# Routing half 0 inside half 1's MLP, a shorter ranking, and fillers paced by scatters: one change to an adaLN block with a mixture of experts

## The reference, cut to what matters

```python
h = _layernorm(x) * (1 + ca) + sa
xn = rmsnorm(h, norm1_w)
left = gelu(xn @ left_W + left_b)
right = rg_lru(causal_depthwise_conv(xn @ right_W + right_b), ...)
x1 = left * right @ out_W + out_b + h
x1n = rmsnorm(x1, norm2_w)
mlp = gelu(x1n @ up1_W + up1_b) * (x1n @ up2_W + up2_b) @ down_W + down_b   # 256 -> 768 -> 256
x = x + ga * (mlp + x1)                                 # called x2 here
h = _layernorm(x) * (1 + cb) + sb                       # called h2 here
logits = h @ gate_w                                     # 8 experts, the best 2 of each token
combined = sum over e of cw[:, e] * (gelu(h @ w1[e] + b1[e]) @ w2[e] + b2[e])   # 256 -> 1024 -> 256
x = x + gb * (combined + h)
```

## Time and profile before

| | us |
|---|---|
| runs shown: lowest, median, highest | 304.69, 307.43, 307.59 |
| the profiled execution, its own time | 304.61 |
| its span (first to last instruction) | 302.9 |
| PE busy | 274.6 (91%) |
| DVE busy | 194.0 (64%) |
| ACT busy | 186.3 (61%) |
| POOL busy | 113.0 (37%) |

### The profile page before, as it was taken

One profiled execution on the slowest core, in us unless ns is written; L12 is line 12 of the kernel. 1 busy time (PEld: TensorE's weight loads), 2 busy tenths in 40 slices (PEclk: granted clock), 3 DMA queues, 4 the chain that ended last, 5 costly groups with the idle time before them and its releaser, 6 DMA issues.

```text
span 302.9 us, 4493 instructions
## 1 busy us (share of the span) xinstructions
PE 274.6 (91%) x1607; PEld 231.5 (76%) x1607; DVE 194.0 (64%) x450; ACT 186.3 (61%) x303; POOL 113.0 (37%) x97
## 2 busy tenths in 40 slices
PE   0799999899999999997798979999999999999980
PEld 0695546378588888785476979999999999999980
DVE  4866737929927365978392676768686867686520
ACT  5166679784296335755851869494949494959200
POOL 6000000000124123507475400838475656657562
PEclk9999999999999999999759999999999999999997
DMA  7970000000004766432135943675758392918133
GB/s 240 381 221 0 2 1 0 0 2 0 0 2 153 233 170 123 86 126 92 54 98 170 285 169 112 210 198 179 232 156 255 126 286 87 280 10 209 26 40 38
DMA packets 32727, 38.26 MB, mean 126 GB/s; under 512 B 7989, under 2 KB 28333, under 8 KB 32685
## 3 DMA queue, kind: packets, MB, share of 16 engines
q1 hardware_dynamic: 26816, 29.90, 31.7%
q0 software_dynamic: 4928, 7.44, 11.0%
q10 hardware_dynamic: 956, 0.59, 0.7%
HBM read 31.96 MB, written 8.90 MB: 135 GB/s over the span
## 4 chain that ended last, share of the span: by engine, by line
PE 41%; ACT 4%; issue 2%; DVE 1%; DMA 1%; POOL 1%; POOLq 1%; another core or an unknown queue 0%; ACTq 0%; DVEq 0%
PE bank L892 17%; PE bank L913 14%; PE bank L657 3%; PE bank L878 2%; PE bank L908 2%; PE bank L907 2%; PE bank L802 1%; DMA out_x<-y_tok,meta 1%; ACT own L1208 1%; POOL out_x L1828 1%; POOLq L188 1%; ACT hT L1086 1%; ACT own_raw L1202 1%; DVE xe_lo L1669 0%; ACT L1105 0%
## 5 line engine op out<-in xcount | busy, mean ns | idle before, releaser
L1828 POOL DMA_INDIRECT out_x<-y_tok,meta x24 | 51.0, 2127 | 50.5 <-DVE y_tok L1691 43.9
L913 PE MATMUL bank<-w_hi,own 128*128 128x256 f32 x256 | 47.9, 285 | 0.0
L892 PE MATMUL bank<-xe_hi,w_hi 128*128 128x320 f32 x128 | 39.7, 310 | 3.3 <-DVE xe_lo L1669 3.3
L1673 DVE TENSOR_TENSOR own<-own_raw,own 128x256 fp32r<-128x256 f32 x64 | 27.2, 425 | 23.3 <-ACT own L1208 17.9
L913 PEld LDWEIGHTS bank<-w_hi,own 128*128 128x128 f32 x256 | 40.4, 191 | 0.4
L1202 ACT ACTIVATE own_raw<-bank,b1c 128x320 f32<-128x320 f32 x64 | 33.9, 529 | 9.7 <-PE bank L892 9.7
L892 PE MATMUL bank<-xe_lo,w_hi 128*128 128x320 f32 x128 | 39.6, 309 | 0.0
L892 PE MATMUL bank<-xe_hi,w_lo 128*128 128x320 f32 x128 | 39.6, 309 | 0.0
L913 PE MATMUL bank<-w_lo,own 128*128 128x256 f32 x128 | 36.2, 283 | 0.0
L1208 ACT ACTIVATE own<-own_raw 128x320 fp32r<-128x320 f32 x64 | 28.7, 460 | 0.0
L1818 POOL DMA_INDIRECT gb_rows<-gb_table,meta x24 | 23.4, 974 | 11.6 <-issue 6.7
(11 more groups left out here) (226 smaller groups left out, 626.9 us busy)
## 6 DMA issues: line engine op xcount, KB each, us to landing
e_raw<-in_L_ffn_w SPq DMA_DIRECT2D x16, 1024.0 KB
x_rows<-in_L_attn_x SPq DMA_DIRECT2D x1, 2560.0 KB
xe_tok<-x_rows SPq DMA_DIRECT2D x8, 256.0 KB
raw_m<-in_L_attn_up_W SPq DMA_DIRECT2D x2, 768.0 KB, 9.9
x_tok<-in_L_attn_x SPq DMA_DIRECT2D x2, 512.0 KB, 5.0
out_x<-x_tok SPq DMA_DIRECT2D x1, 1024.0 KB
wmod<-in_L_wmod SPq DMA_DIRECT2D x1, 768.0 KB, 12.2
raw_m<-in_L_attn_down_W SPq DMA_DIRECT2D x1, 768.0 KB, 13.1
```

Source lines behind the costliest of these rows:

```text
L892: ins = nc.tensor.matmul(bank[b][:, 0:CAP], l, r, start=(c == 0 and t == 0), stop=(c == KD - 1 and t == 2))
L913: ins = nc.tensor.matmul(bank[b][0:n, 0:D], l, r, start=(c == 0 and t == 0), stop=(c == KE - 1 and t == 2))
L1673: nc.vector.tensor_tensor(own_lo[e % 2][:, f, :], own_raw[:, f % 4, 0:whole], own_hi[e % 2][:, f, 0:whole].bitcast(F32), ALU.subtract)
L1828: nc.gpsimd.indirect_dma_start(out_rows, bass.IndirectOffsetOnAxis(ap=ids[0:n, e, k, E:E + 1], axis=0), y_tok[e % 2][0:n, k, :], None, com ...
```

## The change

Six things are changed together.

1. Half 0's routing is written between half 1's `up` products: on TensorE its x2 rows and logits go from behind up(1, 2) to behind up(1, 1), its xh2 turns from behind up(1, 5) to behind up(1, 3), its h2 rows and places from between the two down products to ahead of up(1, 5). On ScalarE the root, the x2 copies, the modulation, exp and the h2 copies go between the gelus 7 to 11; on VectorE stats, norm, logits, choice, weights and slots between `v_of(7)` and `v_of(11)`. The last low part of v moves from GpSimd to VectorE, and w1's low part for expert 0 from behind `v_of(7)` to behind the weights of half 1.
2. The base of x2 (bias and x1, scaled by ga, plus x) is made ahead by `rest_of_x2`, so that behind a down product only one operation a batch is left; the transposes wait for the batch they need.
3. The ranking takes three operations instead of five: a difference, a comparison with `margin` (just below 2^-120 or -2^-120, which settles ties) and the sum.
4. Block 0's x2 rows, its logits and the weights' turn (`turn_weights(0)`) are issued ahead of the last chunk of the last down product.
5. Half 1's xh2 banks hold a batch each instead of a channel block: batch 2 is modulated by VectorE, batch 3 by ScalarE behind exp. Places stand between the two. The scatters' semaphores are one for each 128 tokens, and GpSimd waits for the half of the copied rows that it sends.
6. The 4 and the 30 fillers become 18 in six groups of three, one behind each of half 1's four a scatters and two of its b scatters; the 11 become 10.

```diff
+            def rest_of_x2(hf):
+                for dt in range(KD):
+                    until_drained(("xr", hf, dt))
+                    for q in range(BH):
+                        bb = hf * BH + q
+                        cs = slice(bb * S, (bb + 1) * S)
+                        st.mark(nc.vector.tensor_scalar(tmp[:, 2 + dt, q * S:(q + 1) * S], hT[:, dt, cs], C("down_b", dt), M(GA, dt, bb), ALU.add, ALU.mult))
+                    st.need(st.n)
+                    st.mark(nc.vector.tensor_tensor(xT[:, dt, hs[hf]], xT[:, dt, hs[hf]], tmp[:, 2 + dt, :], ALU.add))
+                return st.n
...
-                    nc.vector.scalar_tensor_tensor(out=tmp[:, 2 + dt, :], in0=ps[:], scalar=C("down_b", dt), in1=hT[:, dt, hs[hf]],
-                                                   op0=ALU.add, op1=ALU.add).then_inc(drained[b], 1)
-                    until_drained(("down", hf, dt))
...
-                        ins = nc.vector.scalar_tensor_tensor(out=xs, in0=tmp[:, 2 + dt, q * S:(q + 1) * S], scalar=M(GA, dt, bb), in1=xs,
-                                                             op0=ALU.mult, op1=ALU.add)
+                        nc.vector.scalar_tensor_tensor(out=xs, in0=ps[:, q * S:(q + 1) * S], scalar=M(GA, dt, bb), in1=xs,
+                                                       op0=ALU.mult, op1=ALU.add).then_inc(drained[b], 1)
...
-                st.mark(nc.vector.tensor_tensor(beats, other, mine, ALU.is_gt))
-                st.link(nc.vector.tensor_tensor(ties, other, mine, ALU.is_equal))
+                st.link(nc.vector.tensor_tensor(beats, other, mine, ALU.subtract))
                 dve.wait_ge(ident_done, 3)
-                st.link(nc.vector.tensor_tensor(ties, ties, before[:].rearrange("p (t e) o -> p t e o", t=1).to_broadcast([P, TH, E, E]), ALU.mult))
-                st.link(nc.vector.tensor_tensor(beats, beats, ties, ALU.add))
+                st.link(nc.vector.tensor_tensor(beats, beats, margin[:].rearrange("p (t e) o -> p t e o", t=1).to_broadcast([P, TH, E, E]), ALU.is_gt))
...
+            down(1, [0])
+
+            def first_rows():
+                x2_and_logits(1, 0)
+                turn_weights(0)
+            down(1, [1], first_rows)
             x2_and_logits(1, 1)
...
+            for n in range(TH):
+                pe.wait_ge(a_scattered[TH + n], 16)
+                stay_busy(("paced", n), any_w1, 3)
+            for n in range(BH):
+                pe.wait_ge(b_scattered[TH + n], 16)
+                stay_busy(("paced", TH + n), any_w1, 3)
...
+            def modulate_last():
+
+                b, ps = full(("xh2", 1, 1))
+                for dt in range(KD):
+                    nc.scalar.activation(hT[:, dt, T - S:T], ps[:, dt * S:(dt + 1) * S], ACT.Identity,
+                                         scale=M(CB, dt, B - 1), bias=M(SB, dt, B - 1)).then_inc(drained[b], 1)
...
             ln_root(4)
             norm2(1)
-            modulate2(1)
             numerators(1)
+            modulate_last()
             keep_h2(1)
+            keep_weights(1)
             keep_x2(1)
```

More of the change, by code:

```diff
@@ L15 @@
 CAP = 320
+TIE = 2.0 ** -120
+BELOW_TIE = TIE * (1 - 2.0 ** -24)
 class Order:
@@ L122, in take_down @@
         for dt in range(KD):
-            order.take(("down", hf, dt))
+            order.take(("down", hf, dt), drains=2)
     def take_x2t(hf):
@@ L155, in adaln_block, with take_at @@
     take_up(1, 1)
-    take_up(1, 2)
     take_x2t(0)
     order.take(("logits", 0))
+    take_up(1, 2)
     take_up(1, 3)
+    take_xh2(0)
     take_up(1, 4)
-    take_up(1, 5)
-    take_xh2(0)
-    order.take(("down", 1, 0))
     take_h2t(0)
     order.take(("places", 0))
-    order.take(("down", 1, 1))
-    take_x2t(1)
+    take_up(1, 5)
+    take_down(1)
+    for p in range(2):
+        order.take(("x2t", 1, p))
     order.take(("logits", 1))
     order.take(("cwT", 0))
-    order.take(("busy", 1), drains=0, bank=6)
-    order.take(("xh2", 1, 0), drains=2, bank=6)
-    order.take(("xh2", 1, 1), drains=2)
-    order.take(("places", 1))
-    order.take(("busy", 3), drains=0, bank=4)
-    order.next = 1
-    order.take(("h2t", 1, 0))
-    order.take(("h2t", 1, 1), bank=4)
-    take_biases(0)
-    order.take(("cwT", 1))
-    take_biases(1)
-    order.take(("busy", 2), drains=0)
+    first_bank = order.next
+    def take_at(key, n, drains=1):
+        order.take(key, drains=drains, bank=(first_bank + n) % 8)
+    take_at(("busy", 1), 0, 0)
+    take_at(("xh2", 1, 0), 0, KD)
+    take_at(("places", 1), 1, 2)
+    take_at(("xh2", 1, 1), 2, KD)
+    take_at(("h2t", 1, 0), 7)
+    take_at(("h2t", 1, 1), 6)
+    take_at(("cwT", 1), 0)
+    take_at(("b2", 0, 0), 1)
+    take_at(("b2", 0, 1), 2)
+    take_at(("b2", 1, 0), 6)
+    take_at(("b2", 1, 1), 7)
+    for n in range(TH + BH):
+        take_at(("paced", n), 3, 0)
     for j in range(4):
@@ L719, in up, with down @@
                 product(("up2", hf, m), wm(1, KD)(m), split_of(n_hi, n_lo, hf), KD)
-            def down(hf, dts=range(KD)):
+            def down(hf, dts=range(KD), between=None):
                 wm_ready(3)
@@ L743, in x2_and_logits, with bank_of @@
             def x2_and_logits(hf, dt):
-                pe.wait_ge(x2_done, KD * hf + dt + 1)
-                for p in range(2):
-                    b, ps = begin(("x2t", hf, p)) if dt == 0 else (order.at[("x2t", hf, p)][0], bank[order.at[("x2t", hf, p)][0]])
+                def bank_of(key):
+                    return begin(key) if dt == 0 else (order.at[key][0], bank[order.at[key][0]])
+                lb, logits = bank_of(("logits", hf))
+                for p in range(BH):
+                    until_drained(("down", hf, dt), p + 1)
+                    b, ps = bank_of(("x2t", hf, p))
                     for q in range(2):
@@ L1161, in all_experts @@
             def all_experts():
-                b, n, _ = order.at[("busy", 2)]
+                b, n, _ = order.at[("paced", TH + BH - 1)]
                 act.wait_ge(filled[b], n)
@@ L1592, in slots @@
                 nc.vector.tensor_scalar(slot_b[:, ts], high[:, ts], -1.0, None, ALU.add).then_inc(slots_done, 1)
+                if hf == NH - 1:
+                    until_drained(("places", hf), 2)
+                    nc.vector.tensor_scalar(overflow[:], most, float(CAP), None, ALU.is_gt).then_inc(overflow_done, 1)
             def w1_lo_of(e):
@@ L1642, in _ @@
             centre(1)
+            b, ps = full(("xh2", 1, 0))
+            for dt in range(KD):
+                nc.vector.tensor_scalar(hT[:, dt, BH * S:(BH + 1) * S], ps[:, dt * S:(dt + 1) * S], M(CB, dt, BH), M(SB, dt, BH), ALU.mult, ALU.add).then_inc(drained[b], 1)
             slots(1)
             weights(1)
+            w1_lo_of(0)
             for hf in range(NH):
```

153 lines of the change are left out of this document (81 added, 72 removed).

## The result

| | before | after |
|---|---|---|
| median of the executions | 307.24 us (304.69 to 307.59, four) | 303.07 us (301.15 to 304.09, four) |
| ratio, 95% interval | | 0.9896, 0.9856 to 0.9936 |
| the profiled execution | 304.61 us, span 302.9 | 303.28 us, span 301.5 |
| mean granted clock in it | 0.976 | 0.958 |

The kernel is faster by 1.0% (0.6 to 1.4). The forecast was 300.8 us, by a shift of 3.9 us. The medians differ by 4.2, the ratio makes 3.2 of 307.2, and the two profiled executions differ by only 1.3. In this document medians are of all executions, and ratios leave out slow ones, more than 1.5% above the kernel's fastest (five of e3's ten, one each of e4, e5 and f2; the profiles of e3 and e5 show such executions).

What follows compares the result with a forecast made beforehand. TensorE-bound expert loop taken as unchanged, so only its start counted: shifts a to e moved the turn of expert 0's rows from 163.88 to 160.0, -3.9; 304.61 - 3.9 = 300.7, said 300.8 us; own range 299 to 302.2, overall 298.3 to 305.3.

Steps and rivals of the forecast that it cites:

- term d: First scatter of half 1 on GpSimd: w1's low part beside it on VectorE costs +1.2 us, bounds 0 and +1.5.
- step e: Load and fillers: load at 155.2, rows in at 160.0, fillers ended before; turn at 160.0 instead of 163.88, -3.9 together.
- a: Until half 1's x2 rows stand in PSUM: pauses and tail change by -0.3 us, bounds -1.0 and +1.5.
- b: Ranking on VectorE: three linked operations instead of five take 1.38 us instead of 2.13, so -0.75.
- c: From the last of `centre` to the weights: exp right behind the normalising, 2.9 us instead of 5.19, so -2.3.
- rival 2: Ahead of slots: the old 3.17 us wait at L1581 comes back, c gives back 2 to 3, 303.2 us; 16%.
- Rival 1, the clock: Granted clock still down when the dense loop starts: 1.7 to 5.1 us lost, taken as 2.6, 303.4 us; 25%.
- Rivals 3 and 4: 3: w1 load or base late, 302.8 us, 6%; 4: down product starved by half 0's slow ranking, 308.7, 5%.
- Rival 5: Slow table switches ahead of gelu 11 on ScalarE: gelu and down product 2.6 us later, 303.3 us; 2%.
- The signs of being wrong: Prediction wrong if the clock is 0.50 behind 160 us, or L1541's last pair ends after 138.

Runs made afterwards that it cites:

- e3: Changed kernel with six times five fillers in one bunch of 30 instead of eighteen waiting for scatters: median 304.86 us, ratio to before 0.9876.
- e4: Changed kernel without the paced fillers (one is left): median 304.63 us, ratio to before 0.9968.
- e5: e1 with 5 fillers behind the turn of expert 0's rows and 8 behind that of expert 1's: median 300.42 us, ratio to before 0.9791.
- f2: Changed kernel with two fillers for each scatter instead of three, 12 in all: median 303.29 us, ratio to before 0.9911.
- f1: The changed kernel itself, unaltered, run and profiled a second time: median 302.01 us, ratio to before 0.9885.
- e7: Changed kernel with both blocks of half 1 modulated on ScalarE and exp behind them again: median 305.23 us, ratio to before 0.9978.
- e2: e1 with expert 1's w1 load held until ScalarE has copied out half 1's weights: median 302.06 us, ratio to before 0.9883.
- e1: Changed kernel with expert 0's w1 low part moved back between the two updates of half 1's xT: median 302.40 us, ratio to before 0.9882.
- e8: Kernel before with only the fillers changed, eighteen in threes waiting for scatters instead of thirty: median 306.46 us, ratio to before 1.0005.
- e6: e1 with the turn of expert 1's rows moved inside expert 0's first layer: median 299.94 us, ratio to before 0.9802.
- g1: e6 with five fillers more behind the turn of expert 0's rows, all eighteen kept: median 299.62 us, ratio to before 0.9801.

## Why the prediction was right and wrong, step by step

Two things failed: the base of the sum, and the size of term d (with step e's claim on the fillers).

**The base of the sum failed.** The prediction took the 3.9 us from the profiled execution of before, 304.61, noted that it "lies at the low end of the runs shown", and then left it there: 300.8 is a figure for an execution without early falls, and it was set beside a median of executions with and without. Against executions without early falls it is nearer: f1's fastest three are 300.9 to 301.6. Taken from the median it would have been 307.4 - 3.9 = 303.5, measured 303.07. The base explains most of the miss, and not all: the ratios give a change of 3.2 and 3.5 us, and the spans without early falls, 302.9 and 299.8, differ by 3.1. Instead of 3.9 the turn moved by 3.4 to 3.5, and 0.3 was lost again behind it, at the end of the span (T to end 139.2 before, 139.5 after). That the low end mattered could be suspected: before's 304.69 stands 2.7 us apart from 307.43 and 307.59, the distance between sets like f1's.

**a** (-0.3, first statistics 137.7): right. 139.40 - 1.71 = 137.69; f1 has 137.77. The pause of 0.47 went, and the new one in the down product was 0.05 instead of 0.3 (the chain's issue piece at 130.33 is 0.04).

**b** (-0.75): right. 142.53 to 143.87 is 1.34, forecast 1.38.

**c** (-2.3): right. From the end of `centre` (144.62) to the weights (147.25) are 2.6 us, forecast 2.9, and no wait ahead of the slots; rival 2 did not come. e7 puts 1.3 of it on exp's place; what ended the old wait at L1581 stays open. The first scatter, without the 1.71, is at 146.15 (forecast 146.75).

**d** (+1.2): mis-sized. From the first scatter to the load 9.50, 9.14 in f1, against 7.28 before: +1.9 to +2.2. The first scatter's step is 2.84 instead of 1.28, so 1.56 for the neighbour, just above my upper bound. In all six profiles that have this neighbour (after, f1, e3, e4, e7, f2) the first scatter ends 0.84 to 0.85 us behind the end of the VectorE operation, in the first at 150.40 against 149.55, although their overlap runs from 1.48 (e4) to 1.91 us (e7). So it waited for the whole rest of the operation, 1.69 us here, and my 1.2, taken from the price of two scatter-adds, was too low. The Trainium skill (SBUF — State Buffer, section SBUF: two separate sides) says that a VectorE operation with two SBUF inputs holds the ports that it shares with GpSimd against a GpSimd instruction that reads SBUF, but it infers that the making of DMA descriptors is not held up by such an operation. The trace agrees with the lock and not with the inference, if making descriptors is what the scatter does on GpSimd: 2.54 us against 0.97. The rest is 0.3 to 0.7. Beside the scatters there now also runs, from 149.58, the 1 MB load of expert 1's w1; I had asked only whether it comes in time, not whom it slows, and e2 gives it 0.5. Yet e1, with neither neighbour, is 0.3 above before too (7.57 against 7.28), so the rest is split only roughly.

**e** (load 155.2, rows in 160.0, turn 160.0): right numbers, by two errors that cancel, which is luck. The load is at 155.65 without the 1.71, 155.38 in f1. The rows are in sooner than 4.8 us behind it: where the turn did wait for them, it came 3.41 (f2), 3.71 (e2), 3.75 (e4) and 4.26 (e7) behind the load; the 4.8 were read off GpSimd's use of `meta`, which lands later. But "three fillers end well before 160 at either clock" was wrong. TensorE starts the fillers late, in the profile after at 155.7, behind 7.1 us of biases at the lower level, in f1 at 153.91, when the first scatter has landed. From there eighteen at 0.36, 6.5 us, follow one another up to the turn with no wait between them: only the first group is paced, and in the profile after not even that one. I had sized the last group and not the queue ahead of it. And a shorter way to the turn was not worth its length: e8, with the paced fillers alone, turns 1.75 us sooner and gains no time.

**Rival 1, the clock** (+2.6, 25%): not in the changed kernel, whose half level ended at 160.28 in one profile and at 158.5 in the other, before the turn in both. But it is what sits right beside it: with six fillers fewer (f2) or the bunch of before replaced (e8) it came, at 1.7 us a fall (half of 3.4). Rivals 3 and 4 did not come: the w1 load landed 5.1 us behind its issue, 154.7, and ScalarE came to it at 156.26 (in f1 it waited 0.9 for it, with 4.3 idle ahead of the first xe_hi); and TensorE has no pause over 0.05 in the down products. Rival 5 did not either: gelu 11 starts 0.01 behind the end of its table load of 1.28 us, and half 1's exp 0.02.

**The signs of being wrong** were set as instants counted from the start, and the early falls shift these. In the profile after both are met (the clock is 0.50 until 160.28, and L1541's last pair ends at 138.81), in f1 neither (158.5, 137.18).

Steps a and b were not undone by themselves; their sizes are read from the two profiles.

## What to carry to other kernels

Before a sum is made against a profiled execution, look at the stretches of the granted clock in the part the change leaves alone, and at the list of times: where they come in sets, the forecast belongs to each set, and a median needs the median's base. Where TensorE waits for data ahead of a dense loop, a shorter wait is worth its length only if the clock survives it, so read the clock behind the wait as well as the wait; here two edits that shortened it by 1.2 and 1.75 us (f2, e8) gained nothing, and closing the next pause as well (e6, g1) gained some 2 us. And for each DMA that a moved step releases, ask both when it must land and what runs beside it.

## What the runs showed of the hardware

- The same code meets the clock's falls in one execution and not in the next: 3.4 us at 0.51 from about 51 us in six of fourteen profiles, 1.00 in the other eight. In the 3.00 us ahead of it TensorE is busy for 2.83 in the profile after, with transposes and matmuls of 4 to 256 columns; in f1, with no fall, it is busy for 3.00. Two such falls, from 51 and 68 us, cost 1.71 us.
- A fall in the dense loop came with all four pauses of 2.14 to 2.50 us, with one of six of 2.05, and with none of 0.82 or less (four).
- A scatter issued on GpSimd while VectorE subtracts one 128x2048 tile from another takes 2.54 us instead of 0.97, in the profiles after and f1 alike (2.53 in e3, 2.33 in e4, 2.76 in e7). Each time it ends 0.84 to 0.85 us behind the end of that operation.
